# Reordering the front of a fused mLSTM and mixture-of-experts kernel, and folding the expert weights by transfer

## The reference

```
xn   = layernorm(x)                                   # per token, no weights
q,k,v = headwise 4x4 block-diagonal products of xn    # 4 heads of 32
i, f = gates from xn (two numbers per head and token)
D    = exp(cumsum(logsigmoid f) differences + i, row-stabilised, causal)
h    = ((q k^T / sqrt(32)) * D, normalised by max(|row sum|, exp(-row max))) v
s    = per-head layernorm(h) * (1 + ln_w)
e    = argmax(xn router_w + router_b)                 # 8 experts, top 1
y    = (a * sigmoid(g)) w2[e] + b2[e],  [a, g] = xn w1[e] + b1[e]   # 128 -> 2x512 -> 128
out  = x + s * silu(y)
```

## Time and profile before

| what | us |
|---|---|
| median of 3 runs (240.56 to 242.08) | 240.97 |
| the profiled execution's own time | 240.99 |
| its span, first to last instruction | 239.2 |
| PE busy | 209.1 |
| DVE busy | 181.8 |
| ACT busy | 136.5 |
| POOL busy | 100.0 |

### The profile page before, as it was taken

How to read it: one execution, slowest core, us unless ns; L and a number is a source line. 1 busy time by engine, 2 the same in 40 slices (tenths; PEclk the granted TensorE clock), 3 DMA queues, 4 the chain that set the end, 5 groups by cost and what they waited for, 6 DMA issues and landing times.

```text
span 239.2 us, 6066 instructions
## 1 busy us (share of the span) xinstructions
PE 209.1 (87%) x1824; PEld 170.8 (71%) x1832; DVE 181.8 (76%) x505; ACT 136.5 (57%) x313; POOL 100.0 (42%) x128
## 2 busy tenths in 40 slices
PE   0688879689999999979999999999999999999650
PEld 0568744335555555559999999999999999986310
DVE  6997378299989986648777988898889789671490
ACT  0276756779788796754555555555555655540110
POOL 7553200027777776000333364425533464366150
PEclk9988999999999999999999999999999999999975
DMA  6999999501441111401097021102101000000994
GB/s 175 266 419 418 282 299 394 221 3 46 146 137 53 49 53 59 115 21 33 15 261 204 26 58 52 55 22 62 44 30 50 28 25 25 26 11 13 251 315 137
DMA packets 29730, 29.30 MB, mean 122 GB/s; under 512 B 3295, under 2 KB 24807, under 8 KB 29697
## 3 DMA queue, kind: packets, MB, share of 16 engines
q1 hardware_dynamic: 26258, 24.59, 33.0%
q0 software_dynamic: 2272, 4.22, 5.4%
q10 hardware_dynamic: 1168, 0.10, 0.4%
HBM read 20.01 MB, written 9.34 MB: 123 GB/s over the span
## 4 chain that ended last, share of the span: by engine, by line
PE 67%; DVE 11%; issue 6%; ACT 5%; DMA 5%; DVEq 1%; SPq 1%; POOL 1%; ACTq 0%; POOLq 0%
PE bank L1195 13%; PE head_bank L1195 13%; PE bank L1204 12%; PE head_bank L1159 5%; PE bank L1169 5%; PE bank L1149 4%; PE head_bank L1052 4%; PE bank L1180 3%; PE bank L1148 3%; DMA xw<-y_tokens 2%; DVE stats L696 2%; PE bank L1037 2%; PE bank L1082 2%; DVE cm L859 2%; PE head_bank L1131 1%
## 5 line engine op out<-in xcount | busy, mean ns | idle before, releaser
L449 POOL DMA_INDIRECT y_tokens<-ffn,idx x39 | 39.2, 1004 | 76.3 <-DVE ffn L992 74.0
L443 POOL DMA_INDIRECT xs_sorted<-xw,pos x32 | 33.0, 1031 | 36.3 <-DVE pos L831 26.9
L1204 PE MATMUL bank<-w_sb,dm 128*128 x312 | 41.3, 275 | 0.5 <-DVE dm L976 0.5
L1195 PE MATMUL bank<-xsT,wc 128*128 128x128 f32 x320 | 39.3, 276 | 0.1
L1204 PEld LDWEIGHTS bank<-w_sb,dm 128*128 128x128 f32 x312 | 38.0, 192 | 0.7 <-issue 0.7
L1195 PEld LDWEIGHTS bank<-xsT,wc 128*128 128x128 f32 x320 | 37.4, 192 | 0.5 <-DVE wc L851 0.3
L1195 PE MATMUL head_bank<-xsT,wc 128*128 128x128 f32 x304 | 37.0, 275 | 0.0
L1195 PEld LDWEIGHTS head_bank<-xsT,wc 128*128 128x128 f32 x304 | 35.4, 192 | 0.0
L859 DVE TENSOR_TENSOR cm<-dm,head_bank 128x1024 f32<-128x1024 f32 (+1 forms) x32 | 29.0, 948 | 6.3 <-ACT dm L586 3.5
L600 ACT ACTIVATE wc<-w_sb 128x512 f32 x39 | 24.6, 630 | 14.3 <-issue 14.3
L586 ACT ACTIVATE dm<-bank 128x512 f32<-128x512 f32 x48 | 26.9, 594 | 4.5 <-PE bank L1149 3.5
(11 more groups left out here) (199 smaller groups left out, 352.0 us busy)
## 6 DMA issues: line engine op xcount, KB each, us to landing
x_sb<-in_L_attn_x SPq DMA_DIRECT2D x16, 256.0 KB, 5.1
w_sb<-in_L_ffn_w SPq DMA_DIRECT2D x8, 512.0 KB, 8.2
wc<-in_L_ffn_w SPq DMA_DIRECT2D x5, 512.0 KB, 17.1
xs_sb<-xs_sorted SPq DMA_DIRECT2D x13, 193.5 KB, 2.8
xs_sorted<-b_sb SPq DMA_DIRECT2D x1, 2048.0 KB, 17.3
xw<-y_tokens SPq DMA_DIRECT2D x8, 256.0 KB, 4.6
out_x<-xw SPq DMA_DIRECT2D x8, 256.0 KB, 3.6
y_tokens<-ffn,idx POOLq DMA_INDIRECT x39, 2.3
```

Of the source, the lines that this page charges most:

```text
L443: pool.indirect_dma_start(xs_dram, bass.IndirectOffsetOnAxis(ap=pos[:, t:t + 1], axis=0), xw[:, t, :], None).then_inc(s_scat, 16)
L449: pool.indirect_dma_start(y_dram, bass.IndirectOffsetOnAxis(ap=idx[:, j:j + 1], axis=0), ys_sb[:, j // CH % 2, j % CH, :], None, bounds_ch ...
L1195: last = pe.matmul(bank[2 * (j % 2) + k][:, c * P:(c + 1) * P], wc[:, j % 3, m:m + P], xsT[:, j % 2, :], start=True, stop=True)
L1204: last = pe.matmul(bank[6 + j % 2][:, 0:D], uT[:, j % 2, c, :], w2_sb[:, bass.ds(e * (HC * D) + c * D, D)], start=(c == 0), stop=(c == HC ...
```

## The change

Statistics of a group's second half are taken after the previous group's Newton steps, and its first half ahead of them. Tiles are dealt out anew (DVE 2, ACT 3, POOL 3 of every 8). Twelve warming matmuls come before PE's wait for the small weights, two before the first transposes, one before the third and the fifth. Four small DMA issues of ACT move behind its first three normalised tiles. All chunks of values are dealt out anew. Query products 0 to 3 are issued before the cumulative sums and 4 and 5 after them; 6 and 7 are copied out by DVE. The selection's first set is copied alone (256 columns), sets 1 and 2 together, set 3 by DVE from another bank. DVE makes `left` of batch 1 and copies the ranks. The exponential of the forget row moves into ACT's batch 1 and its transposes and copy into batch 3. The positions' four steps are spread over batches 0 and 1, the block table's nine steps over batches 2 to 10. The folds leave DVE: the eight last rows are loaded once on 8 partitions, negated on ACT, written to device memory, and added to w1 by eight accumulating DMAs that POOL issues ahead of its scatters. ACT's first two weight copies come one batch earlier, and its load of the sigmoid table one batch later. The diff, cut:

```diff
+            sp.dma_start(last_rows, w1[:, D - 1, :]).then_inc(s_lr, 16)
             for e in range(E):
                 sp.dma_start(w1_sb[:, e, :], w1[e]).then_inc(s_w1, 16)
+            sp.wait_ge(s_neg, 1)
+            sp.dma_start(nrow_dram, last_rows).then_inc(s_nr, 16)
...
-            for e in range(6):
-                sp.dma_start(last_row[e], w1[e, D - 1:D, :].partition_broadcast(P)).then_inc(s_bc[e], 16)
...
-            for e in range(6, E):
-                sp.wait_ge(s_sub, e - 5)
-                sp.dma_start(last_row[e], w1[e, D - 1:D, :].partition_broadcast(P)).then_inc(s_bc[e], 16)
-
-            sp.wait_ge(s_sub, 5)
...
+            pool.wait_ge(s_nr, 16)
+            pool.wait_ge(s_w1, 16 * E)
+            for e in range(E):
+                pool.dma_start(w1_sb[0:P - 1, e, :], nrow_dram[e:e + 1, :].partition_broadcast(P - 1),
+                               accum_op=ALU.add).then_inc(s_sub, 16)
...
-            for n, v in ((0, router_b), (E, bf), (E + NH, bi)):
-                act.dma_start(rb_sb[:, n:n + v.shape[0]], v.partition_broadcast(P)).then_inc(s_small, 16)
-            act.dma_start(gamma[:, :], ln_w.partition_broadcast(P)).then_inc(s_small, 16)
...
-            act.activation(spare[:, 0:1], zeros[:, 0:1], ACT.Sqrt).then_inc(s_dummy, 1)
+            act.preload_act_table_set("sqrt_and_others")
             rsqrt_start(0)
-            rsqrt_start(1)
+            normalised(0)
+            for n, v in ((0, router_b), (E, bf), (E + NH, bi)):
+                act.dma_start(rb_sb[:, n:n + v.shape[0]], v.partition_broadcast(P)).then_inc(s_small, 16)
+            act.dma_start(gamma[:, :], ln_w.partition_broadcast(P)).then_inc(s_small, 16)
             act.wait_ge(s_wT, 1)
             act.activation(wvl[:, 0:D], bank[4][:, P:2 * P], ACT.Copy).then_inc(s_wts, 1)
             act.activation(wvl[:, D + E:VL], bank[4][:, 2 * P:2 * P + 2 * NH], ACT.Copy).then_inc(s_wts, 1)
             act.activation(wqk[:, :], bank[4][:, 0:P], ACT.Copy, scale=float(DH) ** -0.5).then_inc(s_wts, 1)
-            normalised(0)
+            rsqrt_start(1)
             xT_copy(0)
-            rsqrt_start(2)
             xT_copy(1)
             normalised(1)
             evac_vl(0)
-            rsqrt_start(3)
+            act.wait_ge(s_lr, 16)
+            act.activation(last_rows, last_rows, ACT.Copy, scale=-1.0).then_inc(s_neg, 1)
+            rsqrt_start(2)
             xT_copy(2)
             xT_copy(3)
+            evac_vl(1)
+            normalised(2)
             evac_vl(2)
-            normalised(2)
+            rsqrt_start(3)
             xT_copy(4)
-            evac_vl(4)
             xT_copy(5)
             normalised(3)
+            evac_vl(4)
+            xT_copy(6)
             evac_vl(6)
-            xT_copy(6)
-            evac_vl(8)
             xT_copy(7)
             act.preload_act_table_set("natural_log_exp_and_others")
-            evac_vl(10)
+            evac_vl(9)
...
-            evac_q(0)
-            evac_q(1)
+            for c in range(4):
+                evac_q(c)
             act.wait_ge(s_gg2, 1)
             act.activation(gs[:, 0, :], bank[5][0:R, 0:S], ACT.Copy).then_inc(s_gs, 1)
             act.wait_ge(s_grest, 1)
             act.activation(gs[:, 1, :], grest, ACT.Copy).then_inc(s_gs, 1)
-            evac_q(2)
-            evac_q(3)
-
-            def pick_copy(k):
-                act.wait_ge(s_picked, k + 1)
-                act.activation(sel[:, 2 * k:2 * k + 2, :].rearrange("p j s -> p (j s)"), bank[2 + k][:, :], ACT.Copy).then_inc(s_sel, 1)
+            evac_q(4)
+            evac_q(5)
...
+            pick_copy(0, 1)
             act.wait_ge(s_ind, 4)
             act.wait_ge(s_sel, 1)
             right_rows(0, 2)
             right_rows(0, 3)
-            left_rows(1)
-            act.wait_ge(s_fd, 1)
-            act.activation(fl_row, fdiff, ACT.Exp).then_inc(s_flr, 1)
-            evac_q(4)
-            act.wait_ge(s_cnt, 1)
-            act.activation(rank[:, :], bank[4][:, 0:E * T + E + 1], ACT.Copy).then_inc(s_rank, 1)
-            pick_copy(1)
-            evac_q(5)
-            evac_q(6)
-            evac_q(7)
+            pick_copy(1, 2)
...
+            def forget_row():
+                act.wait_ge(s_fd, 1)
+                act.activation(fdiff, fdiff, ACT.Exp).then_inc(s_flr, 1)
...
-                if b + 2 == B - 1:
+                if b == 1:
+                    forget_row()
+                if b == B - 2:
+                    act.wait_ge(s_xone, 1)
+                    evac_xs(0)
                     act.preload_act_table_set("sigmoid_and_others")
...
-                if b == B - 3:
-                    act.wait_ge(s_sub, E)
+                if b == B - 4:
+                    act.wait_ge(s_sub, 16 * E)
                     act.wait_ge(s_b1, 16)
                     act.wait_ge(s_bexp, 1)
                     copy_w(0)
-                if b == B - 2:
+                if b == B - 3:
...
+            for g in range(T // GS):
+                if g >= 1:
+                    link(stats_of(g, GS // 2, GS))
+                else:
+                    link(stats_of(g, 0, GS))
+                variance(g)
+                if g + 1 < T // GS:
+                    stats_of(g + 1, 0, GS // 2)
+                else:
+                    evac_vl(3)
+                newton(g)
+                normalised(g)
+            evac_vl(5)
...
+            dve.wait_ge(s_cs, 1)
+            dve.wait_ge(s_mm, 1)
+            dve.tensor_tensor(fdiff, bank[5][R:P, 0:S], mm, ALU.subtract).then_inc(s_fd, 1)
+            dve.wait_ge(s_picked, 3)
+            dve.tensor_copy(sel[:, 3, :], bank[4][:, 0:S]).then_inc(s_seld, 1)
+            dve.tensor_scalar(left[:, 1, :], sel[:, 0, :], lmask[:, 0, 1:2], lmask[:, 1, 1:2], ALU.mult, ALU.add).then_inc(s_lf1, 1)
+
+            def evac_q(c):
+                dve.wait_ge(s_q, c + 1)
+                dve.tensor_copy(q_all[:, c * 512:(c + 1) * 512], xT_bank[c % 4][:, :]).then_inc(s_qed, 1)
+
+            dve.wait_ge(s_cnt, 1)
+            dve.tensor_copy(rank[:, :], bank[7][:, 0:E * T + E + 1]).then_inc(s_rank, 1)
+            evac_q(NQA)
...
+                places = positions()
                 for b in range(B):
                     weigh(b)
+                    if b == 0:
+                        evac_q(NQA + 1)
                     if b >= 1:
                         outputs(b - 1)
-                    if b == 0:
-                        positions()
-                    if 1 <= b < 4:
-                        for _ in range(3):
-                            step_of = next(blocks, None)
-                            if step_of is not None:
-                                link(step_of)
-                    for _ in range(FOLDS.get(b, 0)):
-                        fold_half(folded[0])
-                        folded[0] += 1
+                    if b < 2:
+                        for place in itertools.islice(places, 2):
+                            link(place)
+                    if 2 <= b < 11:
+                        step_of = next(blocks, None)
+                        if step_of is not None:
+                            link(step_of)
                     if b == B - 4:
...
+                if q in (2, 4):
+                    keep_warm(1, (0, 1, 6, 7)[q % 4])
+                pe.wait_ge(s_xn, q + 1)
+                pe.wait_ge(s_xna, 3 * (q // 2) + (3 if q % 2 else 2))
+                pe.wait_ge(s_xnp, 3 * (q // 2) + (3 if q % 2 else 1))
...
             pe.wait_ge(s_zero, 1)
+            keep_warm(12, 7)
             pe.wait_ge(s_wsmall, 16 * 6)
             pe.wait_ge(s_const, 9)
-            keep_warm(4, 7)
...
+            keep_warm(2, 7)
             transposes(0)
...
-            queries(0)
-            queries(1)
+            for c in range(4):
+                queries(c)
...
-            queries(2)
-            queries(3)
             queries(4)
+            queries(5)
...
-                if j % 2 == 1:
+                if j != 1:
...
-            pe.wait_ge(s_flr, 1)
-            pe.wait_ge(s_grest, 1)
-            for k in range(2):
-                last = pe.transpose(bank[5][:, k * R:(k + 1) * R], fl_row[:, k * P:(k + 1) * P], ident[R:P, R:P])
-            last.then_inc(s_flp, 1)
+            pe.wait_ge(s_qe, 4)
...
-            queries(7)
-            pe.wait_ge(s_tm, 1)
-            pe.wait_ge(s_rank, 1)
             pe.wait_ge(s_sel, 2)
+            pe.wait_ge(s_seld, 1)
+            pe.wait_ge(s_grest, 1)
+            pe.wait_ge(s_fd, 1)
             scores(0)
             log_decay(0, 2)
+            pe.wait_ge(s_rank, 1)
+            queries(7)
             for m in range(3):
                 log_decay(1, m)
```

More of the change, by code:

```diff
@@ L43, in mlstm_moe_block @@
     NV = (T + 2) // 3
-    DVE_VL = (1, 3, 5, 7, 9)
+    DVE_VL = (3, 5, 7, 8, 10)
     GS = 8
+    FORGET = 3
+    PICK_BANK = (2, 3, 3, 4)
+    PICK_COL = (0, 0, S, 0)
     NBS = B // 4
@@ L205, in mlstm_moe_block @@
         s_b1 = sem("s_b1")
```

(38 more changed lines are left out.)

91 lines of the change are left out of this document (31 added, 60 removed).

## The result

| | us |
| --- | --- |
| before, median of 4 runs beside it | 241.5 |
| after, median of 4 runs (232.43 to 234.42) | **232.9** |
| ratio, with its 95% interval | 0.968 (0.964 to 0.972) |
| forecast | 233.3 (231.0 to 237.8) |
| profiled execution after: time, span | 232.86, 231.0 |

The account below looks back on a forecast made before the run. PE was taken as full in experts and attention, the front as a chain of waits. Terms to hidden of block 1 (-3.65, -4.4, +0.1, +0.3) gave -7.7: 240.99 - 7.7 = 233.3 us, range 231.0 to 237.8.

Parts of the forecast that it names:

- First stretch: From the start to the cumulative sums: they start at 30.3 instead of 33.95, -3.65 us.
- the 1.9 for ACT's four DMA issues: In the front: ACT issues four moved small DMAs after normalising three tiles, 0.45 each, about 1.9 us, until 11.6.
- Second stretch: From the cumulative sums to the scores of batch 1: 12.0 us instead of 16.4, -4.4.
- Attention: Fourteen steps to scores(15): fold removal 0, block table 0.5 back, forget row's exponential +0.4 and transposes +0.2; sum +0.1 us.
- the -0.5 for the block table: Attention, batches 2 and 3, where the block table's steps came three at a time: 0.5 us of PE's idle back.
- Passage: From scores(15) to hidden(1): moves worth 1.5 us are eaten by waiting for sorted rows; hidden(1) at 100.4 against 108.07.
- the wait of 1.9: Passage: PE asks for the sorted rows at 94.1, they land at 96.0, so it waits 1.9 us.
- rival 2: Passage is freer: scatters run closer together and the 1.9 us wait goes, 231.4 us; chance 0.05.
- Experts and end: The expert blocks and the stretch after the last hidden: not touched, forecast 0.
- a front that gives half for the clock: PE at the slow clock again, ACT's DMA issues longer: 3 to 5 us of gain stay, 236 to 238; chance 0.17.
- 3: POOL still writing accumulations when positions are ready, delaying scatters: 250 us at 5 each, 274 at 8; chance 0.10.
- Rival 4: Folds arrive late, all eight transfers on one DMA engine, ending at 205 against 81: about 357 us; chance 0.02.

Follow-up runs that it names:

- e1: The changed kernel with the folds back on DVE (16 subtractions in batches 1 to 10): 244.98 us, ratio 0.965 to the kernel before on the same, slower chip.
- e3: The changed kernel with the first stretch as before: 249.13 us, ratio 0.983 to the kernel before on the same, slower chip.
- e2: The kernel before with only the folds changed, to eight adding transfers of negated rows: 251.5 us, ratio 0.994 to the kernel before on the same, slower chip.
- e9: The changed kernel with the forget row's exponential in ACT's batch 2 instead of 1: 231.93 us, ratio 0.962 to the kernel before.
- e4: The changed kernel with the eight fold transfers as plain copies, addition left out: 246.34 us, ratio 0.971 to the kernel before on the same, slower chip.
- e11: The changed kernel with each fold transfer split in four, 32 adding transfers of 1 KB rows: 236.64 us, ratio 0.982 to the kernel before.
- e8: The changed kernel with no warming matmul at all: 234.82 us, ratio 0.971 to the kernel before.
- e7: The changed kernel with warming as before, four matmuls behind the waits for small weights and constants: 234.33 us, ratio 0.975 to the kernel before.
- e12: The changed kernel with ACT's four small transfers issued ahead of its table load: 245.58 us, ratio 0.966 to the kernel before on the same, slower chip.

## Why the prediction was right

Right in the total and in the two large terms, with misses that partly cancel. That the total is within 0.5 is in part luck: the first stretch and the passage came out 2.0 better than forecast, attention, experts and the end 1.5 worse.

- **First stretch** (-3.65 forecast, -4.38 measured). Newton(0) ended at 8.63 (8.4 forecast). The step that failed is the 1.9 for ACT's four DMA issues ahead of the weight products' copy: I laid them end to end behind the normalisations, and they ran beside these, in time in which ACT waited for PE anyway. The first copy came at 12.15 for 12.3, by luck, for the chain was another: warming to 9.4, products, the two warming matmuls ahead of the transposes (10.54 to 11.67, while the tiles were ready at 10.1), transposes. Whether those two can go was not run. The rest of the gain is ACT's full stretch, from there to its last copy 12.6 instead of 13.2 (a chunk of values takes it 0.45 to 0.5 and not 0.6, a root 0.1 and not 0.2); from that copy to the cumulative sums 4.83, as forecast (4.8).
- **Second stretch** (-4.4, -4.40). Selection 34.35 (34.9), log-decay(0) 37.07 (37.8), scores(0) 37.59 (38.5), scores(1) 41.58 (42.3): each 0.5 to 0.9 early, by what the first stretch gained. No run undoes this stretch alone, but it takes 12.01 in e1 (old folds) and in e3 (old first stretch), and 16.41 in e2 (new folds, everything else old): so the gain belongs to the new order in it. Which of the moves gives how much was not separated.
- **Attention** (+0.1, +0.34). e9 separates the terms: without the forget row there, steps 2 and 3 take 7.22 where they took 7.73, the -0.5 for the block table; the exponential cost 0.58 and not 0.4, as PE waits for the last of three instructions behind it; the transposes 0.27 for 0.2. The folds' removal gave nothing in itself (e1), as costed.
- **Passage** (+0.3, -1.00). The step that failed: the wait of 1.9. I took the scatters' 41.47 and the load's 3.65 behind the last one from the kernel before. The 41.47 held 8 stretched scatters, six of them beside a fold, and these are gone; 39.66 is 31 periods of 1.27 and a slower start. The load was issued 2.34 behind the last scatter (2.3 to 2.4 in e1 to e4 too, in e1 with the old folds; 3.65 stands in the one trace of the kernel before, and why is open). With 1.2 from the earlier positions that is 4.3, so the rows were there by 91.7 for a PE that asks at 93.6; e11 puts the slack at 2.4. This was rival 2, which I gave 0.05: its evidence, 0.96 without a fold beside it, stood in the rows, and deserved to be the forecast.
- **Experts and end** (0, +1.24). Forecast at 0, not touched, and yet longer. The experts' +0.46 doesn't go with the transfers: e1 without them takes 103.7, e2 with them 103.2, the others 103.6 to 103.9. One step of blocks is 3.40 for 3.15 and one 2.99 for 2.79, each beside a DVE instruction of 2.6 to 2.7 us, which in the kernel before are 2.7 and 2.4 long; what makes them so long is open. The end is 28.3 to 28.8 in the variants with the changed front and the transfers (e11's aside). The end's work is unchanged (last hidden to DVE's last addition 22.14 before, 22.19 after); the 0.7 lies behind it, where SP closes the program. SP's waits there, of before, after and e1 (total, times, longest):

```profile
SPq L71 <- PEq L71: 1.0, 1, 1.0
```

```profile
SPq L75 <- PEq L75: 3.0, 1, 3.0
```

```profile
SPq L76 <- PEq L76: 1.9, 1, 1.9
```

With the folds back on DVE the wait is 1.9 and the stretch 27.6; in e2 2.6 and 27.9; with four times the transfers 3.8 and 30.2. So in these traces the stretch grows with their number (the wait alone doesn't tell: e1's is 0.9 longer than before, its stretch isn't), and how a transfer that landed at 57 can do that, no run shows.
- **Rivals.** 1, a front that gives half for the clock: no, but its danger was real (e8). 3: no, at 0.90 a transfer (7.19 in all, where the lower bound had 10) POOL was done at 30 for 46; e11 shows the price beyond the cover. 4: no, the folds were done by about 57, wanted at 81. The eight adding transfers never went to one engine. (Rival 4's worst case counts one reading for each, 181; read twice, as in its sentence before, it would be 362.)

## What to carry to other kernels

Before you forecast that a freed wait is eaten by the next one, remove from the next one's length what the same change takes away beside it: the scatters' pace in the old trace had the folds in it. Instructions that an engine issues cost nothing while its next arithmetic waits for somebody else, so place each on the timeline and don't add it to the sum. And warming matmuls ahead of the first wait cost nothing here, twelve of them, while four behind it cost 1.4 us.

## What the runs showed of the hardware

**TensorE's clock.** In the kernel before, PE warmed up, then sat idle for 1.03 ahead of 14.22, and the granted clock went from 1.00 to 0.50 (its lower level, 1.2 GHz) in 16:18. e2 and e3 have the same idle 1.03 there and fall to 0.60 and 0.80 in 14:16; in e7, with the same four warming matmuls, the transposes follow the products without a gap and it stays at 1.00. In the changed kernel it is 1.00 throughout the front. In e8 the matmuls ran at the lower level's durations to about 17 while the row of the granted clock says 1.00 (first the row of the kernel before at 0.50, then e8's):

```profile
16.00:18.00 2.00, 2.00 (x11) 1.99 (x10) 1.97 (x14) 1.91 (x6) 0.48 (x4) 0.50 1.02 420
```

```profile
12.00:14.00 2.00, 2.00 (x10) 1.70 (x9) 1.57 (x8) 1.31 (x5) 1.42 (x6) 1.00 0.95 340
```

So at the start of a kernel the durations tell the level, not the column.

**127 partitions.** By the Trainium skill, DMA: Bandwidth & Descriptors, "Why a DMA increments its semaphore by 16 and not by 1", a DMA of 127 partitions goes to one engine, some direct copies from GpSimd excepted; here all 16 were full (share 1.06 in the window from 29.57, of which 0.80 the queue of the adding transfers alone, where eight transfers on an engine each could make 0.50 at most), so either that exception covers adding copies or it isn't needed. By Collectives: The Full Stack, "The bandwidth ceiling", a step that adds reads two sources and runs at half the rate of a copy; here a packet took 1.4 times as long.

**An interruption on two chips.** In e4:

```profile
59.56 0.96 POOL L451 DMA_INDIRECT xs_sorted<-xw,pos  x1 [0.30 <-issue]
...
60.78 1.25 PE L1197 MATMUL bank<-spread,uTs 128*128 128x132 f32 x4 [8.83 <-issue]
...
63.94 0.43 DVE L883 COPY u_all<-bank 128x264 f32<-128x264 f32 x1 [8.85 <-remote]
```

PE and ACT stand for 8.8 us from 51.9 and 51.5, DVE for as long from 55.1, waiting for nothing that the profile explains, while POOL goes on every 1.26. One step of attention takes 14.07 for it and the next 5.77, with the granted clock at 0.50 in 60:65. In e3 and e12 PE stands for 7.5 and 6.7; in e1 and e2 the same comes in two parts. The packets of the two instruction queues that landed at 56 and 57 in the changed kernel landed at 63 and 65 in e4. The Trainium skill, Runtime: NRT & Kernel Launch, "Instruction fetch mechanics", says that fetching is mostly hidden; this may be a case where it isn't, but no run tested it.
